# Row sums of the two longest query blocks in one accumulator each, in a two-layer transformer kernel on one Trainium2 core

## The chip, the cores and the metric

The kernel runs on one core of one Trainium2 chip. The metric is the time of one execution on the device, in microseconds (us). The kernel before was timed in three runs: 1879.6, 1879.7 and 1876.36 us, so the median is 1879.6 us. One more execution was recorded by the hardware profiler; it took 1874.3 us, and the span from its first to its last instruction is 1872.6 us.

## The reference, cut to what matters

The program computes two layers (causal attention and a mixture of experts, then a selective scan and a second mixture of experts) on 4 sequences of 1024 tokens of width 128, in float32. Only the attention of the first layer is touched. It has 16 query heads of width 64 that share 4 key and value heads (4 query heads to one key head):

```python
q = (hidden_states @ Wq).reshape(b, s, H, D).transpose(0, 2, 1, 3)     # b=4, s=1024, H=16, D=64
k = (hidden_states @ Wk).reshape(b, s, HKV, D).transpose(0, 2, 1, 3)   # HKV=4
v = (hidden_states @ Wv).reshape(b, s, HKV, D).transpose(0, 2, 1, 3)
q, k = _apply_rope(q, cos, sin), _apply_rope(k, cos, sin)
scores = jnp.einsum('bkgqd,bkpd->bkgqp', qg, k) * scale
scores = jnp.where(causal, scores, jnp.float32(-1e+30))
probs = jax.nn.softmax(scores, axis=-1)
out = jnp.einsum('bkgqp,bkpd->bkgqd', probs, v).reshape(b, H, s, D)
```

The part that the change concerns is the denominator of the softmax: for each query the sum of `exp(score - max)` over all keys up to its own.

## The kernel before, in words

**Groups.** Attention is done in 16 groups, one for each sequence and key head; a group has 4 query heads. Queries and keys are cut into 8 blocks of 128. A first pass (`s1`) makes all scores to find each row's maximum (matmuls L700 on TensorE, maximum L838 on VectorE). A second pass works on *units* `(qb, kb)`, one query block by one key block with `kb <= qb`, for the 4 heads at once, so a tile is 128 keys by 512 columns (4 heads by 128 queries). There are 36 units in a group. The second pass of group g runs beside the first pass of group g+1, and beside the rotary embedding of groups g+1 and g+2.

**One unit.** `s2`: two matmuls make the scores less the maximum (L714, L715 on TensorE, into one of 6 banks called `ring`). `exp2`: ScalarE takes the exponential into one of 9 buffers `prob` (L924); on the diagonal (`kb == qb`) GpSimd then zeroes what is above it (`affine_select`, L963). `pv`: TensorE multiplies with `v` into `ps_o` (L731).

**Row sums.** Units are gathered in *runs*. Within a run GpSimd adds the `prob` tiles: the first add makes `acc` from two tiles (L975), each later one adds a tile to `acc` (L978); there are 2 buffers `acc`. When the run is complete, TensorE multiplies `acc` with ones, once for each pair of heads (two products, L743, a step called `sum`), and adds into `ps_l`. After the last run of an odd query block ScalarE takes the logarithm and the negative exponential of `ps_l` (L928, L932, step `norm`), and VectorE multiplies `ps_o` with it (L851, step `take`). A run is a part of a *batch*: query blocks 0 and 1 form one batch, blocks 2 to 5 one each, block 6 has two batches, key blocks 0 to 3 and 4 to 6, and block 7 has two, 0 to 3 and 4 to 7. Before, a run never went beyond its batch, so query blocks 6 and 7 had two runs each. A group had 10 runs.

**Rotary embedding.** Six steps `rot` for each group (r = 0 to 5; r = 0 and 3 are keys, the others queries). TensorE projects (L682), VectorE multiplies by the cosine and swaps neighbours (L816, L817), GpSimd multiplies by the sine and adds (L945, L947). The step `split` that belongs to it makes a rounded copy on ScalarE (L903 for keys, L906 for queries) and the rest on VectorE (L827, L830). The DMAs of the queries into place follow it.

**What sets the order.** `attention_plan` gives each step a time by rule and sorts all steps by it; each engine then walks the same sorted list and issues its share in that order, without ever passing a step that waits. The second pass is spread from g+1.0 to g+1.97 in proportion to costs: 0.5 for each unit, and for the products of the batch before `0.45 * len(late) + 0.3`, where `late` holds its `pv` steps and its `sum` steps. `exp2` is placed 0.012 behind its `s2`. The steps `rot` and `split` have fixed times that don't depend on these costs. Banks of `ring` go to each step by the same times: the bank whose last holder was due earliest. Before TensorE writes to a bank it waits for the step that read that bank last. The other waits that matter: `pv` of a diagonal unit waits for the `affine_select`, and `sum` waits for the last add of its run.

Of the kernel before, what the change touches and what calls it, by code (L numbers as in the profile page):

```python
# [329 lines left out]
def load_attention(e, a, tensors, x, early, late):  # L330
# [18 lines left out]
NQB = SEQ // P  # L349
# [6 lines left out]
BATCHES = [[(0, 0), (1, 0), (1, 1)]] + [[(qb, kb) for kb in range(qb + 1)] for qb in range(2, 6)] + [  # L356
    [(qb, kb) for kb in part] for qb, parts in ((6, (range(4), range(4, 7))), (7, (range(4), range(4, 8)))) for part in parts]
# [13 lines left out]

def runs():

    out = []
    for batch in BATCHES:
        for qb in dict.fromkeys(qb for qb, _ in batch):
            out.append([unit for unit in batch if unit[0] == qb])
    return out


RUNS = runs()
RUN_OF = {unit: n for n, run in enumerate(RUNS) for unit in run}


def attention_plan():

    order = []

    def spread(steps, start, end):

        total = sum(cost for cost, *_ in steps)
        used = 0.0
        for cost, *together in steps:
            at = used + (MIDDLE * cost if len(together) > 1 else 0.0)
            order.extend((start + (end - start) * at / total, step) for step in together)
            used += cost  # L400

    for g in range(GROUPS):
        for r in range(ROTS):
            c, j = divmod(r, 1 + NPAIR)
            at = g + (ROT0, ROT1)[c] + ROT_STEP * j
            order.append((at, ("rot", g, r)))
            order.append((at + ROT_LAG, ("split", g, r)))
        order.append((g + 0.55, ("v", g)))
        for c in range(NCH):
            first = []  # L410
            for h in range(G):
                for qb in range(c * QPC, (c + 1) * QPC):
                    first.append(((qb + 1) * 0.14 + 0.3, ("s1", g, h, qb)))
            spread(first, g + (0.0, S1_HALF)[c], g + (S1_HALF, 1.0)[c])
        order.append((g + S1_HALF + 0.06, ("rows", g, 0)))
        order.append((g + 1.03, ("rows", g, 1)))
        second, late = [], []
        for j, batch in enumerate(BATCHES):
            for i, unit in enumerate(batch):
                second.append((0.5, ("s2", g) + unit))  # L420
                if late and i == min(PV_AFTER + (j == 1), len(batch) - 1):
                    second.append((0.45 * len(late) + 0.3, *late))
                    late = []
            late += [("pv", g) + unit for unit in batch] + [("sum", g, n) for n in dict.fromkeys(RUN_OF[unit] for unit in batch)]
        spread(second, g + S2_START, g + S2_END)
        order.extend((g + S2_END + LATE, step) for step in late)
        if g % HKV == 0 and g:

            for n in range(TPB // 4):
                at = g - 1.9 + 0.25 * n  # L430
                order += [(at, ("xnorm", g // HKV, n)), (at + 0.05, ("turn", g // HKV, n)), (at + 0.07, ("xout", g // HKV, n))]
        if g == GROUPS - 1:

            order.append((g + OUT, ("again", g // HKV)))
        elif g % HKV == HKV - 1:
            order.append((g + OUT - 0.001, ("again", g // HKV)))
            for n in range(TPB):
                at = g + OUT + 0.03 * n
                order.append((at, ("out", g // HKV, n)))
                order.append((at + 0.016, ("add", g // HKV, n)))  # L440
                order.append((at + 0.0199, ("stats", g // HKV, n)))
    order.append((0.5, ("gates",)))
    order += [(1.0 + 0.9 * (i - TPB) / (TILES - TPB), ("xstat", i)) for i in range(TPB, TILES)]
    order.append((1.95, ("xscale",)))

    for at, step in list(order):
        if step[0] == "s2":
            order.append((at + LAG_EXP2, ("exp2",) + step[1:]))
        elif step[0] == "sum" and RUNS[step[2]][-1][0] == RUNS[step[2]][-1][1] and RUNS[step[2]][-1][0] % 2:
            pair = RUNS[step[2]][-1][0] // 2  # L450
            order.append((at + LAG_NORM, ("norm", step[1], pair)))
            order.append((at + LAG_TAKE, ("take", step[1], pair)))
    return sorted(order, key=lambda item: item[0])


def attention(nc, sems, a, h_t, attn_t, wo, ident, eps, zeros, stats, mv, mod_t, gates, slots_in, slots_zero):
    x = h_t[:, :].rearrange("p (t n) -> p t n", n=HID)
    timed = attention_plan()
    plan = [step for _, step in timed]
    with ExitStack() as ctx:  # L460
# [2313 lines left out]
```

## Time and profile before

| | |
|---|---|
| median of three runs | 1879.6 us (1876.36 to 1879.7) |
| the profiled execution | 1874.3 us, span 1872.6 us |
| mean granted TensorE clock | 0.914 |
| attention, from the first to the last second-pass matmul | 75.6 to some 1092 us |
| busy in the span | PE 1552.5, DVE 1187.0, ACT 791.1, POOL 1264.9 us |

PE is TensorE, DVE VectorE, ACT ScalarE, POOL GpSimd. Names in a row are `out<-in`. Because matmuls are pipelined, the durations of neighbouring ones overlap; how long one really takes is read from the distance between starts. Times in rows are counted from the start of the span. A wait is named by the engine and line that released it.

### The profile page before, as it was taken

Reading aid. Unit: us, or ns where it says so; the run is one execution under the profiler, and the core shown is the slowest. Engines: PE = TensorE matmul, PEld = TensorE weight load, DVE = VectorE, ACT = ScalarE, POOL = GpSimd, SP = SyncE. Lnnn points to the kernel's source line nnn. Section 1 sums busy time; section 2 is a strip of 40 time slices with the busy share of each in tenths; the row PEclk is TensorE's granted clock in tenths of the full one; section 3 lists DMA queues with packets and bytes.
Section 4 is the critical chain, followed back from the end, with each engine's and each line's share of the span. In section 5 each row is a group of like instructions: output and inputs, shape, how many; then the busy total and the mean of one; then the engine's idle time right before and its main releaser. Section 6 shows DMA issues by size and latency. Waiting matters only on the chain. (4 is left out here: it accounts for less than half of the span.)

```text
span 1872.6 us, 26570 instructions
## 1 busy us (share of the span) xinstructions
PE 1552.5 (83%) x8882; PEld 1072.4 (57%) x8882; DVE 1187.0 (63%) x2509; ACT 791.1 (42%) x1347; POOL 1264.9 (68%) x1073
## 2 busy tenths in 40 slices
PE   5799999999999999999999989999965664356970
PEld 3455556755656765567656568888831231235970
DVE  6866676576666567666666235576659989952134
ACT  2245444344443354443444433322267855423320
POOL 5588998798888788887888753110026667658476
PEclk7799999999999999999999999999978876667995
DMA  6333322221122122122121020000036555405333
GB/s 176 70 80 79 69 56 47 46 68 35 40 63 69 29 52 68 35 52 63 35 58 45 12 67 1 1 1 1 1 101 157 143 124 139 115 26 173 98 93 85
DMA packets 93560, 125.30 MB, mean 67 GB/s; under 512 B 13664, under 2 KB 53492, under 8 KB 93424
## 3 DMA queue, kind: packets, MB, share of 16 engines
q1 hardware_dynamic: 89328, 115.58, 24.9%
q0 software_dynamic: 4096, 8.02, 1.5%
q8 instruction: 72, 1.18, 0.3%
q14 instruction: 64, 0.52, 0.1%
HBM read 56.56 MB, written 16.78 MB: 39 GB/s over the span
## 5 line engine op out<-in xcount | busy, mean ns | idle before, releaser
L838 DVE CUSTOM_DVE_ANT_0 ring<-ring,mask 128x128 f32<-128x128 f32 (+7 forms) x512 | 383.7, 769 | 186.0 <-PE ring L700 185.6
L924 ACT ACTIVATE prob<-ring 128x512 f32<-128x512 f32 x576 | 315.1, 597 | 296.6 <-PE ring L715 293.0
L978 POOL TENSOR_TENSOR acc<-acc,prob 128x512 f32<-128x512 f32 x272 | 353.3, 1299 | 72.1 <-ACT prob L924 48.3
L731 PE MATMUL ps_o<-prob,v 128*64 128x256 f32 x2304 | 282.0, 386 | 4.2 <-issue 3.8
L700 PE MATMUL ring<-k,x 128*128 128x512 f32 (+3 forms) x768 | 250.0, 405 | 36.4 <-ACT prob L924 22.1
L714 PE MATMUL ring<-x,k 128*128 128x512 f32 x576 | 258.6, 449 | 24.5 <-DVE neg_m L838 15.4
L715 PE MATMUL ring<-x,k 128*128 128x512 f32 x576 | 229.2, 398 | 0.0
L700 PEld LDWEIGHTS ring<-k,x 128*128 128x128 f32 x768 | 136.6, 197 | 143.9 <-ACT prob L924 50.5
L731 PEld LDWEIGHTS ps_o<-prob,v 128*64 128x64 f32 x2304 | 154.2, 137 | 106.3 <-issue 38.5
L975 POOL TENSOR_TENSOR acc<-prob 128x512 f32<-128x512 f32 x144 | 184.4, 1281 | 8.8 <-ACT prob L924 7.4
L945 POOL TENSOR_TENSOR other<-other,sin 128x512 f32<-128x512 f32 x96 | 136.3, 1420 | 57.1 <-DVE other L817 56.6
L714 PEld LDWEIGHTS ring<-x,k 128*128 128x128 f32 x576 | 109.3, 190 | 99.4 <-issue 44.0
L2375 POOL TENSOR_TENSOR m_hc<-m_st,m_crep 128x1024 f32<-128x1024 f32 x42 | 98.8, 2353 | 53.6 <-DVE m_st L2140 47.9
L947 POOL TENSOR_TENSOR rot<-rot,other 128x512 f32<-128x512 f32 x96 | 129.1, 1344 | 7.5
L1765 POOL TENSOR_TENSOR first_h<-first_h,e_scaled 128x512 f32<-128x512 f32 x8 | 10.3, 1285 | 174.4 <-DVE e_scaled L1647 174.4
L715 PEld LDWEIGHTS ring<-x,k 128*128 128x128 f32 x576 | 110.0, 191 | 19.9 <-issue 7.3
L830 DVE TENSOR_TENSOR rot<-rot,other 128x512 fp32r<-128x512 f32 x64 | 73.2, 1143 | 69.5 <-ACT other L906 69.5
L1633 DVE TENSOR_TENSOR e_both<-e_silu,ps_moe 128x512 f32<-128x512 f32 x88 | 60.4, 687 | 87.9 <-PE ps_moe L1477 69.4
L1717 ACT ACTIVATE e_silu<-ps_moe 128x512 f32<-128x512 f32 x88 | 52.6, 598 | 134.9 <-PE ps_moe L1477 132.2
L963 POOL TENSOR_SCALAR_AFFINE_SELECT prob<-prob 128x512 f32<-128x512 f32 x128 | 91.4, 714 | 25.8 <-ACT prob L924 24.7
L816 DVE TENSOR_TENSOR rot<-ring,cos 128x512 f32<-128x512 f32 x96 | 66.3, 690 | 58.1 <-PE ring L682 57.7
L2594 POOL DMA_INDIRECT c_got<-slots_out,f_slot x64 | 66.5, 1040 | 45.7 <-issue 39.8
(322 smaller groups left out, 3068.5 us busy)
## 6 DMA issues: line engine op xcount, KB each, us to landing
x<-other SPq DMA_DIRECT2D x256, 128.0 KB, 2.3
m_x_rep<-u_mem SPq DMA_DIRECT2D x59, 512.0 KB, 4.6
x<-rot SPq DMA_DIRECT2D x128, 128.0 KB, 2.3
slots_in<-zeros SPq DMA_DIRECT2D x2, 2048.0 KB, 8.7
slots_out<-wo SPq DMA_DIRECT2D x16, 256.0 KB, 2.5
gate<-slots_in SPq DMA_DIRECT2D x11, 256.0 KB, 3.2
m_x_rep<-u_mem SPq DMA_DIRECT2D x10, 256.0 KB, 4.2
e_w<-in_w SPq DMA_DIRECT2D x3, 704.0 KB, 6.9
```

The costliest lines, as they stand in the source:

```text
L700: mm = e.matmul(ps[:, c0:c1], x1[g % 2][:, h, qs], k1[g % 3][:, c0:c1], start=True, stop=True)
L714: e.matmul(banks(step, BANK), k1[g % 3][:, ks], x1[g % 2][:, :, qs], start=True, stop=False)
L715: e.matmul(banks(step, BANK), k2[g % 3][:, ks], x2[g % 2][:, :, qs], start=False, stop=True).then_inc(s2_pe.sem, 1)
L731: mm = e.matmul(ps_o[s * D:(s + 1) * D, qb % 2 * 2 * P:(qb % 2 + 1) * 2 * P], v[g % 2][:, kb, :], prob[i % NPROB][:, s * 2 * P:(s + 1) * 2 ...
L838: e.tensor_tensor_reduce(ps, ps, mask_1[:, SEQ - n:SEQ], 1.0, -3.0 * NEG, ALU.add, ALU.min, neg_m[g % 2][:, c, h, qb % QPC:qb % QPC + 1]). ...
L924: e.activation(prob[i % NPROB][:, :], banks(("s2",) + key, BANK), ACT.Exp, scale=-1.0).then_inc(s2_exp.sem, 1)
L945: e.tensor_tensor(other[i][:, :], other[i][:, :], sin[:, cc], ALU.mult).then_inc(rotated.sem, 1)
L947: e.tensor_tensor(rot[i][:, :], rot[i][:, :], other[i][:, :], ALU.add).then_inc(rotated.sem, 1)
L963: e.affine_select(tile[:, :], tile[:, :], [[0, G], [1, P]], ALU.is_ge, 0.0, base=0, channel_multiplier=-1).then_inc(causal.sem, 1)
L975: e.tensor_tensor(total[:, :], first[:, :], tile[:, :], ALU.add).then_inc(summed.sem, 1)
L978: e.tensor_tensor(total[:, :], total[:, :], tile[:, :], ALU.add).then_inc(summed.sem, 1)
L2375: e.tensor_tensor(hc[(b * NG + g) % NHC][:, :], st[r][:, :], crep[b % 2][:, :], ALU.mult).then_inc(hc_pool.sem, 1)
```

## The change

Runs no longer follow the batches: each query block has one run over all its key blocks. Batches stay as they are, and so do the `pv` steps. The step `sum` is placed with the batch that holds the run's last unit. A group then has 8 runs, and in query blocks 6 and 7 units (6, 4) and (7, 4), which used to open a second run, are added to the accumulator that is already there.

```diff
 def runs():
 
-    out = []
-    for batch in BATCHES:
-        for qb in dict.fromkeys(qb for qb, _ in batch):
-            out.append([unit for unit in batch if unit[0] == qb])
-    return out
+    return [[(qb, kb) for kb in range(qb + 1)] for qb in range(NQB)]
...
-            late += [("pv", g) + unit for unit in batch] + [("sum", g, n) for n in dict.fromkeys(RUN_OF[unit] for unit in batch)]
+            late += [("pv", g) + unit for unit in batch] + [("sum", g, n) for n in (RUN_OF[unit] for unit in batch if unit == RUNS[RUN_OF[unit]][-1])]
```

The program has fewer TensorE instructions and more on GpSimd, and because `len(late)` is smaller by one for two batches, all second-pass steps of a group move a little in time against the steps with fixed times. (Lines behind the first hunk have numbers smaller by 4: the first add is L971 after the change, the later ones L974, `affine_select` L959, the rotation L941 and L943, the exponential L920, `split` L902.)

GpSimd in one group, from the first add of query block 6 to its last. L945 and L947 are the rotation steps 0, 1 and 2 (by the number behind `other`); `acc0` is the sum of key blocks 0 to 3, `acc1` that of 4 to 6. Before:

```order
L975 TENSOR_TENSOR acc0<-prob3,prob4 128x512
L945 TENSOR_TENSOR other0<-other0,sin 128x512
L947 TENSOR_TENSOR rot0<-rot0,other0 128x512
L978 TENSOR_TENSOR acc0<-acc0,prob5 128x512
L945 TENSOR_TENSOR other1<-other1,sin 128x512
L947 TENSOR_TENSOR rot1<-rot1,other1 128x512
L978 TENSOR_TENSOR acc0<-acc0,prob6 128x512
L975 TENSOR_TENSOR acc1<-prob7,prob8 128x512
L963 AFFINE_SELECT prob0<-prob0 128x512
L978 TENSOR_TENSOR acc1<-acc1,prob0 128x512
L945 TENSOR_TENSOR other2<-other2,sin 128x512
L947 TENSOR_TENSOR rot2<-rot2,other2 128x512
```

The same place now:

```order
L941 TENSOR_TENSOR other0<-other0,sin 128x512
L943 TENSOR_TENSOR rot0<-rot0,other0 128x512
L971 TENSOR_TENSOR acc0<-prob3,prob4 128x512
L974 TENSOR_TENSOR acc0<-acc0,prob5 128x512
L941 TENSOR_TENSOR other1<-other1,sin 128x512
L943 TENSOR_TENSOR rot1<-rot1,other1 128x512
L974 TENSOR_TENSOR acc0<-acc0,prob6 128x512
L974 TENSOR_TENSOR acc0<-acc0,prob7 128x512
L941 TENSOR_TENSOR other2<-other2,sin 128x512
L943 TENSOR_TENSOR rot2<-rot2,other2 128x512
L974 TENSOR_TENSOR acc0<-acc0,prob8 128x512
L959 AFFINE_SELECT prob0<-prob0 128x512
```

Rotation 0 now stands ahead of the first add, there is one more add (`prob7`), and rotation 2 stands ahead of the last two adds of the block (the second of them follows the row shown last).

ScalarE in the same group, around the split of rotation 2 (`other2<-rot2`). `prob1`, `prob2` and `prob3` are the exponentials of units (7, 0), (7, 1) and (7, 2). Before:

```order
L906 ACTIVATE other1<-rot1 128x512
L924 ACTIVATE prob1<-ring 128x512
L924 ACTIVATE prob2<-ring 128x512
L906 ACTIVATE other2<-rot2 128x512
L924 ACTIVATE prob3<-ring 128x512
```

The same place now:

```order
L902 ACTIVATE other1<-rot1 128x512
L920 ACTIVATE prob1<-ring 128x512
L902 ACTIVATE other2<-rot2 128x512
L920 ACTIVATE prob2<-ring 128x512
L920 ACTIVATE prob3<-ring 128x512
```

The split of rotation 2 has moved ahead of the exponential of (7, 1).

## Rows read from the trace of the kernel before

**Rows 1.** The page: busy tenths in 40 slices of the span.

```profile
PE   5799999999999999999999989999965664356970
POOL 5588998798888788887888753110026667658476
```

**Rows 2.** Busy time by stretch: stretch, length, engines (us, instructions), clock, DMA share, GB/s.

```profile
528.70:590.40 61.70, 57.77 (x336) 37.03 (x335) 41.48 (x93) 28.09 (x54) 55.36 (x47) 1.00 0.23 52
```

**Rows 3.** Waits of TensorE in the attention, 75 to 1095 us: total, times, longest.

```profile
PE ring L700 <- ACT prob L924: 22.1, 33, 2.1
PE ring L714 <- DVE neg_m L838: 15.4, 14, 1.1
PE ring L714 <- ACT prob L924: 9.0, 13, 0.9
```

**Rows 4.** Timeline of TensorE, the second pass of group 7: start, duration, engine, instruction.

```profile
531.53 0.60 PE L743 MATMUL ps_l<-acc,v_one 128*64 128x256 f32 x4
...
542.12 0.44 PE L700 MATMUL ring<-k,x 128*128 128x384 f32 x1 [1.11 <-ACT prob L924]
...
560.18 0.40 PE L714 MATMUL ring<-x,k 128*128 128x512 f32 x1
560.42 0.39 PE L715 MATMUL ring<-x,k 128*128 128x512 f32 x1
...
581.67 0.50 PE L714 MATMUL ring<-x,k 128*128 128x512 f32 x1 [0.85 <-ACT prob L924]
...
583.50 0.50 PE L714 MATMUL ring<-x,k 128*128 128x512 f32 x1 [1.10 <-DVE neg_m L838]
...
593.21 0.60 PE L743 MATMUL ps_l<-acc,v_one 128*64 128x256 f32 x4
...
605.54 0.60 PE L743 MATMUL ps_l<-prob,v_one 128*64 128x256 f32 x4
605.97 0.60 PE L743 MATMUL ps_l<-acc,v_one 128*64 128x256 f32 x4
```

**Rows 5.** Timeline of GpSimd, the same group, query blocks 6 and 7.

```profile
566.06 1.28 POOL L945 TENSOR_TENSOR other<-other,sin 128x512 f32<-128x512 f32 x1 [0.82 <-DVE other L817]
...
568.65 1.27 POOL L978 TENSOR_TENSOR acc<-acc,prob 128x512 f32<-128x512 f32 x1
569.88 1.75 POOL L945 TENSOR_TENSOR other<-other,sin 128x512 f32<-128x512 f32 x1
...
585.00 1.27 POOL L975 TENSOR_TENSOR acc<-prob 128x512 f32<-128x512 f32 x1 [0.21 <-ACT prob L924]
...
590.83 0.64 POOL L963 TENSOR_SCALAR_AFFINE_SELECT prob<-prob 128x512 f32<-128x512 f32 x1 [0.44 <-ACT prob L924]
591.55 1.28 POOL L978 TENSOR_TENSOR acc<-acc,prob 128x512 f32<-128x512 f32 x1
592.79 1.73 POOL L945 TENSOR_TENSOR other<-other,sin 128x512 f32<-128x512 f32 x1
```

**Rows 6.** Timeline of ScalarE: the two splits that it waits for.

```profile
539.83 0.63 ACT L906 ACTIVATE other<-rot 128x512 fp32r<-128x512 f32 x1 [2.98 <-POOL rot L947]
...
580.50 0.63 ACT L906 ACTIVATE other<-rot 128x512 fp32r<-128x512 f32 x1 [2.89 <-POOL rot L947]
```

**Rows 7.** Timeline of VectorE: two of its splits.

```profile
569.39 1.08 DVE L827 SCALAR_TENSOR_TENSOR k<-rot,k 64x512 fp32r<-64x512 f32 x1
...
592.27 1.10 DVE L827 SCALAR_TENSOR_TENSOR k<-rot,k 64x512 fp32r<-64x512 f32 x1
```

**Rows 8.** Timeline of GpSimd at the end of group 14's and in group 15's second pass.

```profile
1046.50 0.63 POOL L963 TENSOR_SCALAR_AFFINE_SELECT prob<-prob 128x512 f32<-128x512 f32 x1 [1.73 <-ACT prob L924]
...
1083.93 2.70 POOL L978 TENSOR_TENSOR acc<-acc,prob 128x512 f32<-128x512 f32 x2
...
1089.66 0.63 POOL L963 TENSOR_SCALAR_AFFINE_SELECT prob<-prob 128x512 f32<-128x512 f32 x1 [0.37 <-ACT prob L924]
```

**Rows 9.** Timeline of TensorE: the last `sum` of the attention.

```profile
1091.69 0.65 PE L743 MATMUL ps_l<-acc,v_one 128*64 128x256 f32 x4 [0.69 <-POOL acc L978]
```

## The prediction

> **What bounds the kernel now.** I read the page first. In the slices of the attention (the 2nd to the 24th, some 75 to 1092 us) TensorE shows 9 tenths nearly everywhere and GpSimd 7 to 9 [rows 1]: the busiest engine is TensorE, but GpSimd is close behind it. Next comes one group by itself. The second passes of groups 1 to 13 are alike in order and nearly alike in time, so I take group 7: between its neighbours' last sums lie 593.21 - 531.53 = 61.68 us [rows 4]. In about that stretch TensorE is busy 57.77 us, GpSimd 55.36 us, and the clock is full (1.00) [rows 2]. GpSimd has 6.3 us that are not busy, and part of that is no slack: two adds that follow each other in one accumulator are a chain, and two of them take 2.70 us [rows 8], so the second starts 2.70 - 1.28 = 1.42 us behind the first, where an add that need not wait for the one before is followed after 569.88 - 568.65 = 1.23 us [rows 5].
>
> Then the waits of TensorE. In the whole attention they are small, and the largest are of one make: for ScalarE's exponential and for VectorE's maximum, 22.1, 15.4 and 9.0 us, the last two 14 and 13 times, once a group [rows 3]. In group 7 they stand at 542.12, 581.67 and 583.50 [rows 4]. What is behind them is seen on ScalarE: before both places it stood still for 2.98 and 2.89 us at a `split`, for GpSimd's rotation (L947) [rows 6], and the exponential that TensorE wanted was queued behind that split. So TensorE's pauses are GpSimd's backlog. One more number matters most. The last add of query block 7 ends at 591.55 + 1.28 = 592.83, and TensorE takes up that `sum` at 593.21 [rows 4, 5]. That is 0.38 us of slack on TensorE's own in-order queue. From rotation 0, which GpSimd begins at 566.06 after a wait for VectorE, to that add, GpSimd works through 26.77 us with hardly a pause [rows 5]. The group is a loop of two stretches: GpSimd from rotation 0 to the last add, then TensorE from the last `sum` to the next rotation 0 (61.68 - 26.77 - 0.38 = 34.53 us).
>
> **What is removed.** Two `sum` steps a group, 32 in all. One takes 605.97 - 605.54 = 0.43 us of TensorE [rows 4], so 32 x 0.43 = 13.8 us. Both lie in the batches of query blocks 6 and 7, that is inside GpSimd's stretch, where TensorE has to wait for the last add anyway. Their worth there is nothing as long as GpSimd is the later one; if it is not, it is 13.8 us.
>
> **What is added and moved, per group.** All of this is in GpSimd's stretch:
> - Two adds, for units (6, 4) and (7, 4), both in the middle of a chain: 2 x 1.42 = 2.84 us.
> - Rotation 0 now stands ahead of the first add of block 6. Before, that add filled the time in which GpSimd waited for VectorE; now it stands behind: +1.24 us. The bounds are 0 (if rotation 0 comes so early that nothing idles) and 1.42.
> - Pauses that are filled: 0.21 us before the add at 585.00, of which 0.07 is more than a chain's step, and 0.44 + 0.04 before the mask at 590.83 [rows 5]: -0.55 us.
> - The split of rotation 3 is on VectorE at 592.27 for 1.10 us, and GpSimd's instruction beside it takes 1.73 us in place of 1.28 [rows 5, 7]. With GpSimd late, that 0.45 us falls on an add before the last `sum`: +0.45 us.
>
> Sum of the stretch: 2.84 + 1.24 - 0.55 + 0.45 = 3.98 us, so 30.75 us in place of 26.77.
>
> What the loop gives back: rotation 0 is projected one unit earlier on TensorE (one `s2` less ahead of it, two matmuls at 560.42 - 560.18 = 0.24 us [rows 4]), 0.47 us. The slack of 0.38 shrinks to the least handover that `sum` steps show, some 0.05: 0.33 us. And the early wait at 542.12 hangs on rotation 5, which comes 0.33 us later against the last `sum` and 0.45 us earlier by the port that it no longer shares there: -0.12 us. The loop grows by 3.98 - 0.47 - 0.33 - 0.12 = 3.06 us.
>
> Two waits also change, inside the stretch. ScalarE's split of rotation 2 now stands ahead of the exponential of (7, 1), and by the rule for the banks TensorE's `s1` of head 3, block 4 now needs that bank; TensorE will stand there for 2 to 3 us. On the other side rotation 2 stands ahead of the last two adds of block 6, its split comes sooner, and the two waits at 581.67 and 583.50 should go. I cost both at nothing: GpSimd's backlog covers them, since it has five adds of block 7 in hand. Without that cover they are worth up to +1 us, or -1.95 us (0.85 + 1.10). The diagonal `pv` and the `sum` of block 6 will wait for the later adds; covered in the same way.
>
> The other places: 14 second passes (groups 0 to 13) have rotations in them, so 14 x 3.06 = 42.8 us. Group 14 has none, and GpSimd waited 1.73 us for its last exponential [rows 8], so there the adds are hidden and 0.86 us of products is saved. In group 15 GpSimd goes from add to add, and the last `sum` waits 0.69 us for it [rows 9]: two adds and two more chain steps, less a pause of 0.37 + 0.04 [rows 8], 2.84 + 0.38 - 0.41 = 2.8 us. Sum: 42.8 - 0.9 + 2.8 = 44.7 us. From the profiled execution's 1874.3 us this gives 1919.0 us. The median of the runs shown is 5.3 us above that execution, which would give 1924.3. I take 1922 us.
>
> The rotation's port in more detail. A split of 569.39 to 570.47 overlaps the add of 568.65 to 569.92, and the rotation behind that add, begun at 569.88, takes 1.75 us where it takes 1.28 alone [rows 5, 7]. In the Trainium skill, "SBUF — State Buffer", section "SBUF: two separate sides", the pair of ports that VectorE and GpSimd share is a lock: who starts first holds it for a whole instruction, and a VectorE instruction with two inputs in SBUF takes part. By that rule, the trace agrees: the split waits for the add and the rotation for the split. It makes each split beside a busy GpSimd cost about the same wherever it falls; if the price were instead spread over what runs beside it, the loop would grow by some 2.6 us, not 3.1.
>
> **The rivals.**
> *TensorE stays the bound.* It is busy 57.77 of 61.70 us against 55.36 [rows 2]. If GpSimd's 2.6 us more fit in its 6.3 us not busy, 13.8 us are saved, and with rotation 2 moved ahead the two late waits may go too (15.4 + 9.0 us [rows 3]): 1866 down to 1841 us. Against it: the slack of 0.38 us at the last `sum`, and that most of GpSimd's 6.3 us lie in front of rotation 0 or in handovers. The Trainium skill, "Perfetto Trace Analysis", section "Identifying the Most-Contended Engine", has the engine with the highest occupancy as the one to relieve, though it warns that TensorE's busy share misleads; taken simply, it would side with this rival.
> *Only the added work counts.* The moved rotation costs nothing, because the order before and after lets VectorE's part come early enough. Then the loop grows by 2.84 - 0.55 - 0.33 = 1.96 us, with group 15: 14 x 1.96 + 2 = some 29 us, 1903 to 1909 us.
> *GpSimd also starves.* The long stop of TensorE behind the split of rotation 2 makes the exponentials of block 7 late, so that GpSimd's backlog is used up and the filled pauses of 0.55 us come back with 0.5 to 1 us more. The loop grows by 4.1 to 4.6 us: 1935 to 1945 us. It decides once `s2` of (7, 3) comes later than GpSimd's add of (7, 2) ends.
> *Nothing to be seen.* Slack lost and products saved cancel.
> That the change doesn't do what it says is out: the order shows the adds and the moves in every group.
>
> **Chances.** My forecast 0.56, only the added work 0.20, starving 0.10, TensorE the bound 0.10, nothing 0.04. About 0.2% (3.8 us) is what a measurement can tell from no change. Faster 0.10, same 0.04, slower 0.86. The forecast's own range is 1911 to 1933; with the second case and a part of the third it is 1893 to 1938.
>
> **What would show it.** In the profile after: GpSimd with 448 adds in place of 416 and hardly a pause from rotation 0 to the last add, some 30.7 us; the last `sum` of each group waiting for GpSimd (L974), which happens in few groups before; the distance between last sums near 64.7 us; TensorE's share lower in all slices of the attention and nothing changed behind 1140 us but a shift. A wait of TensorE's first-pass matmul (L696) for an exponential near the end of block 6, and none at the later `s2`. I am wrong if the last `sum` still finds its accumulator ready, or if the distance is below 61.7 us.

## The result, and the profile after

The changed kernel takes 1914.91 us (median of four runs, 1914.21 to 1915.85) against 1879.18 us of before in the same comparison: a ratio of 1.0194, with a 95% interval of 1.0181 to 1.0207. It is slower by some 36 us; 1922 us had been predicted, in a range of 1911 to 1933. Its profiled execution has a span of 1913.2 us, 40.6 us more than that of before, where the working had come to 44.7 us. (The profiled execution of before lay 5 us below its median; that of after did not, hence 36 in the medians and 41 between the profiles.)

The same two lines of the page as in [rows 1], now after the change:

```profile
PE   5899889989988989998998989999976655455970
POOL 5588998798889688888788773201016666657476
```

TensorE now dips to 8 tenths again and again; GpSimd is as full as it was. The timeline of TensorE in group 7 (start, duration, engine, instruction), to lay beside [rows 4]:

```profile
548.48 0.65 PE L739 MATMUL ps_l<-acc,v_one 128*64 128x256 f32 x4 [0.97 <-POOL acc L974]
...
596.89 0.56 PE L696 MATMUL ring<-k,x 128*128 128x512 f32 x2 [3.01 <-ACT prob L920]
597.38 2.28 PE L727 MATMUL ps_o<-prob,v 128*64 128x256 f32 x12
599.45 1.12 PE L739 MATMUL ps_l<-acc,v_one 128*64 128x256 f32 x4
600.50 0.80 PE L710 MATMUL ring<-x,k 128*128 128x512 f32 x1
...
611.41 0.65 PE L727 MATMUL ps_o<-prob,v 128*64 128x256 f32 x4 [0.93 <-POOL prob L959]
612.76 0.65 PE L739 MATMUL ps_l<-acc,v_one 128*64 128x256 f32 x4 [0.69 <-POOL acc L974]
```

The last sums are 612.76 - 548.48 = 64.28 us apart (61.68 before), and both wait for GpSimd's last add; before, TensorE came 0.38 us after it. The pauses of 0.85 and 1.10 us are gone, and a pause of 3.01 us stands in front of the first-pass matmul of head 3, block 4. (It stands there in groups 1, 3, 7 and 11. In the other nine of groups 1 to 13 it comes a little later, 2.8 to 2.9 us for the mask of block 6, which is the first line of the waits below.) GpSimd in the same group, beside [rows 5]:

```profile
582.01 1.28 POOL L941 TENSOR_TENSOR other<-other,sin 128x512 f32<-128x512 f32 x1 [1.35 <-DVE other L813]
583.37 1.28 POOL L943 TENSOR_TENSOR rot<-rot,other 128x512 f32<-128x512 f32 x1
584.60 1.28 POOL L971 TENSOR_TENSOR acc<-prob 128x512 f32<-128x512 f32 x1
586.02 1.56 POOL L974 TENSOR_TENSOR acc<-acc,prob 128x512 f32<-128x512 f32 x1
...
590.14 2.98 POOL L974 TENSOR_TENSOR acc<-acc,prob 128x512 f32<-128x512 f32 x2
...
602.35 4.12 POOL L974 TENSOR_TENSOR acc<-acc,prob 128x512 f32<-128x512 f32 x3 [0.40 <-ACT prob L920]
...
610.27 1.09 POOL L959 TENSOR_SCALAR_AFFINE_SELECT prob<-prob 128x512 f32<-128x512 f32 x1
611.44 1.26 POOL L974 TENSOR_TENSOR acc<-acc,prob 128x512 f32<-128x512 f32 x1
```

From rotation 0 at 582.01 to the end of the last add at 612.70 are 30.69 us, where there were 26.77. The rest of the loop, from the last sum to rotation 0, is 582.01 - 548.48 = 33.53 us (34.53 before). The groups of L974 and L971 in this stretch of the profile, with 21 and 7 adds, against 17 and 9 before in a group:

```profile
L974 POOL TENSOR_TENSOR acc<-acc,prob 128x512 f32<-128x512 f32 x21 | 27.4, 1303 | 4.4 <-ACT prob L920 2.6
L971 POOL TENSOR_TENSOR acc<-prob 128x512 f32<-128x512 f32 x7 | 8.9, 1275 | 0.1
```

The waits of TensorE in the attention (total, times, longest), beside [rows 3]:

```profile
PE ps_o L727 <- POOL prob L959: 35.3, 17, 2.9
PE ring L696 <- ACT prob L920: 30.6, 31, 3.2
PE ps_l L739 <- POOL acc L974: 20.4, 28, 1.0
```

Two of the three now name GpSimd directly. One thing the prediction had not foreseen. The columns of a stretch are its length, the busy times, and then TensorE's clock; here are a piece of group 7 and one of group 8, each behind its long pause:

```profile
598.00:601.50 3.50, 3.50 (x17) 1.68 (x13) 1.45 (x4) 0.00 (x0) 3.32 (x3) 0.51 0.87 197
676.00:683.50 7.50, 6.74 (x19) 4.21 (x20) 2.65 (x6) 2.16 (x4) 6.49 (x7) 0.54 0.43 98
```

The clock is about half in both (1.2 GHz). So it is in each of groups 1 to 13, for 3.4 us in five of them and for 6.8 us in eight. It was not always full before the change either: in groups 4, 5, 8, 9 and 12 it is half for 3.4 us behind the late pauses, here in group 4:

```profile
394.30:397.70 3.40, 3.40 (x9) 2.20 (x9) 1.70 (x4) 1.19 (x2) 2.54 (x3) 0.51 0.68 156
```

In the change the `sum` at 599.45 lasts 1.12 us, and 0.60 at full clock [rows 4].

### The profile page after: what moved, and what is told of

The parts are those of the page before. It is cut to its first block and busy times, and to the rows that moved or that the text cites. A ratio compares the mean times of both kernels' runs of the same rounds, so it can differ in the third digit from the quotient of the medians.

```text
span 1913.2 us, 26364 instructions
## 1 busy us (share of the span) xinstructions
PE 1559.2 (82%) x8754; PEld 1077.8 (56%) x8754; DVE 1185.6 (62%) x2509; ACT 794.4 (42%) x1347; POOL 1301.4 (68%) x1105
## 5 line engine op out<-in xcount | busy, mean ns | idle before, releaser
L974 POOL TENSOR_TENSOR acc<-acc,prob 128x512 f32<-128x512 f32 x336 | 439.6, 1308 | 76.2 <-ACT prob L920 46.8
L920 ACT ACTIVATE prob<-ring 128x512 f32<-128x512 f32 x576 | 318.6, 596 | 310.5 <-PE ring L711 307.8
L727 PE MATMUL ps_o<-prob,v 128*64 128x256 f32 x2304 | 291.9, 393 | 39.8 <-POOL prob L959 35.3
L710 PE MATMUL ring<-x,k 128*128 128x512 f32 x576 | 276.0, 479 | 0.1
L696 PE MATMUL ring<-k,x 128*128 128x512 f32 (+3 forms) x768 | 235.2, 386 | 41.3 <-ACT prob L920 30.6
L711 PE MATMUL ring<-x,k 128*128 128x512 f32 x576 | 235.8, 409 | 0.0
L696 PEld LDWEIGHTS ring<-k,x 128*128 128x128 f32 x768 | 142.4, 199 | 124.2 <-ACT prob L920 43.7
L941 POOL TENSOR_TENSOR other<-other,sin 128x512 f32<-128x512 f32 x96 | 123.8, 1289 | 68.7 <-DVE other L813 68.6
L710 PEld LDWEIGHTS ring<-x,k 128*128 128x128 f32 x576 | 114.0, 198 | 80.4 <-issue 59.5
L971 POOL TENSOR_TENSOR acc<-prob 128x512 f32<-128x512 f32 x112 | 144.4, 1289 | 1.5
L943 POOL TENSOR_TENSOR rot<-rot,other 128x512 f32<-128x512 f32 x96 | 128.0, 1334 | 7.5
L711 PEld LDWEIGHTS ring<-x,k 128*128 128x128 f32 x576 | 114.6, 199 | 25.4 <-issue 13.3
L959 POOL TENSOR_SCALAR_AFFINE_SELECT prob<-prob 128x512 f32<-128x512 f32 x128 | 94.8, 741 | 22.6 <-ACT prob L920 21.5
L847 DVE TENSOR_TENSOR attn_t<-ps_o,inv_l 128x512 f32<-128x512 f32 x64 | 44.1, 689 | 93.0 <-ACT inv_l L928 93.0
```

The source lines that it names most:

```text
L696: mm = e.matmul(ps[:, c0:c1], x1[g % 2][:, h, qs], k1[g % 3][:, c0:c1], start=True, stop=True)
L710: e.matmul(banks(step, BANK), k1[g % 3][:, ks], x1[g % 2][:, :, qs], start=True, stop=False)
L711: e.matmul(banks(step, BANK), k2[g % 3][:, ks], x2[g % 2][:, :, qs], start=False, stop=True).then_inc(s2_pe.sem, 1)
L727: mm = e.matmul(ps_o[s * D:(s + 1) * D, qb % 2 * 2 * P:(qb % 2 + 1) * 2 * P], v[g % 2][:, kb, :], prob[i % NPROB][:, s * 2 * P:(s + 1) * 2 ...
L920: e.activation(prob[i % NPROB][:, :], banks(("s2",) + key, BANK), ACT.Exp, scale=-1.0).then_inc(s2_exp.sem, 1)
L941: e.tensor_tensor(other[i][:, :], other[i][:, :], sin[:, cc], ALU.mult).then_inc(rotated.sem, 1)
```

## The experiments

For each run the two parts of the loop in group 7 are read as above: GpSimd's stretch, the slack at the last sum, TensorE's stretch, and their sum. The kernel before has 26.77 + 0.38 + 34.53 = 61.68, the change 30.69 + 0.05 + 33.53 = 64.28 (rounded; the slack of 0.05 us is 612.76 less the end of the last add). Where a text below speaks of a mean, it is that of groups 1 to 13 of the profiled execution, read in the same way.

**The order alone** (e1_order_only). On the kernel before:

```diff
-                    second.append((0.45 * len(late) + 0.3, *late))
+                    n_late = len([s for s in late if s[0] == "pv" or RUNS[s[2]][-1][0] == RUNS[s[2]][-1][1]])
+                    second.append((0.45 * n_late + 0.3, *late))
```

> The kernel before with the order of the change and nothing else: the runs stay ten to a group (no add more on GpSimd, the products stay), but the cost of the late steps is counted as in the change, so all steps and banks stand where the change puts them. Theory (a loop of GpSimd's stretch from rotation 0 to the last add, and TensorE's from there to the next rotation 0): after the change these were 30.69 and 33.53 us; without two chained adds (2 x 1.42) the loop is some 61.4 to 61.8 us as before (61.7), so 1875 to 1885 us. Rival 'the moves are what costs' (rotations ahead of adds, the split ahead of the exponential of (7, 1)): most of the 36 us stays, 1900 to 1915 us.

Measured: 1870.74 us against 1877.31, ratio 0.9967 (0.9954 to 0.9979), 6.6 us faster than before, and outside both ranges. Timelines of TensorE and GpSimd:

```profile
529.22 0.44 PE L744 MATMUL ps_l<-acc,v_one 128*64 128x256 f32 x2 [0.73 <-POOL acc L979]
...
562.80 1.27 POOL L946 TENSOR_TENSOR other<-other,sin 128x512 f32<-128x512 f32 x1 [1.36 <-DVE other L818]
...
588.84 1.76 POOL L979 TENSOR_TENSOR acc<-acc,prob 128x512 f32<-128x512 f32 x1
590.66 0.65 PE L744 MATMUL ps_l<-acc,v_one 128*64 128x256 f32 x4 [0.73 <-POOL acc L979]
```

27.80 + 0.06 + 33.58 = 61.44 us. The moves cost GpSimd's stretch 1.0 us and give back 0.95 us of TensorE's and 0.3 us of slack: they are a small gain, not the loss. A part of the 6.6 us is the clock, which is half in one of groups 1 to 13 here, and in five before.

**The adds alone** (e2_adds_only). On the change:

```diff
-                    second.append((0.45 * len(late) + 0.3, *late))
+                    n_late = len(late) + (late[0][2] >= 6 and late[0][3] == 0)
+                    second.append((0.45 * n_late + 0.3, *late))
```

> The change with the order of before: eight runs to a group (two adds more on GpSimd, two pairs of products less), but the cost of the late steps counted as before, so nothing moves. Theory: GpSimd's stretch is 26.77 + 2.84 + up to 0.5 for chain steps and ports - 0.5 for a filled pause = some 29.4 us, TensorE's stays 34.5, the loop is 63.9 us, in all 1906 to 1915 us. Rival 'the moves are what costs': 1870 to 1885 us, since 13.8 us of products are gone and GpSimd has 6 us not busy in a group.

Measured: 1911.16 us, ratio 1.0177 (1.0161 to 1.0193): inside the theory's range, 34 us slower than before. Timelines:

```profile
547.01 0.60 PE L740 MATMUL ps_l<-acc,v_one 128*64 128x256 f32 x4
...
581.56 1.28 POOL L942 TENSOR_TENSOR other<-other,sin 128x512 f32<-128x512 f32 x1 [0.84 <-DVE other L814]
...
609.63 1.29 POOL L975 TENSOR_TENSOR acc<-acc,prob 128x512 f32<-128x512 f32 x1
```

The next last sum starts at 611.30. So 29.36 + 0.38 + 34.55 = 64.29 us: with nothing moved, nearly the whole loss is there.

**The products back** (e3_products_back). On the change, ahead of the `pv` of (6, 3) and (7, 3):

```diff
+                    if (qb, kb) in ((6, 3), (7, 3)):
+                        if qb == 6 and o_order[g, 3]:
+                            e.wait_ge(inv_act.sem, o_order[g, 3])
+                        for s in range(2):
+                            e.matmul(ps_l[s * D:(s + 1) * D, qb % 2 * 2 * P:(qb % 2 + 1) * 2 * P], v_one[:, :],
+                                     prob[i % NPROB][:, s * 2 * P:(s + 1) * 2 * P], start=True, stop=True)
```

> The change with the two pairs of products with ones issued again in their old places (their result is overwritten by the real ones), 32 pairs of 0.43 us. Theory: they lie in GpSimd's stretch, so only group 14 and nothing else grows: 1914 to 1918 us. Rival 'TensorE's work sets the pace': 1915 + 13.8 = 1929 us.

Measured: 1917.93 us, ratio 1.0218 (1.0202 to 1.0234), 3 us above the change, not 14. (The change was timed in another comparison; by the two ratios, 1.0218 and 1.0194, it is 4.5 us.) In the profiled executions the last sum of the attention comes 1132.06 - 1130.83 = 1.2 us later, 0.9 of them in group 14; the other 2 us lie behind the attention, where nothing was edited. In group 7 the distance is 64.33 us with the products and 64.28 without. So the 13.8 us of products that the change removes were worth some 1 to 5 us.

**The adds left out** (e4_adds_out). On the change: `NO_ADD = ((6, 4), (7, 4))`, and GpSimd passes over these units.

```diff
-                    if unit == run[0]:
+                    if unit == run[0] or unit in NO_ADD:
                         continue
```

> The change without the two added adds: the tiles of units (6, 4) and (7, 4) are left out of the row sums; the order and the removed products stay as in the change. Theory: GpSimd's stretch 30.69 - 2.84 = 27.9 us, loop 61.4 us, and the removed products give something only in groups 14 and 15: 1872 to 1880 us. Rival 'TensorE's work sets the pace': 13.8 us less than the run with the order alone.

Measured: 1879.22 us, ratio 1.0003 (0.9991 to 1.0016). The two adds a group are worth 36 us by this (44 us against the run with the order alone, and 34 us in the order of before). The rival, 13.8 us below the run with the order alone, is out: it is 8 us above. In group 7 the loop is 28.57 + 0.06 + 33.56 = 62.19 us, 0.75 us more than with the order alone. There the exponential of (7, 3) came 0.9 us later, in a stretch in which TensorE's clock was half, behind a pause of 1.80 us; with the order alone that pause was 1.42 us and the clock stayed up.

This run has a comparison within itself. Groups 7 and 11 have the same steps in the same order, and all but the same pause at the same place (1.80 and 1.78 us). Behind it the clock fell in one and not in the other:

```profile
577.83 0.56 PE L699 MATMUL ring<-k,x 128*128 128x512 f32 x2 [1.80 <-ACT prob L923]
842.37 0.56 PE L699 MATMUL ring<-k,x 128*128 128x512 f32 x2 [1.78 <-ACT prob L923]
```
```profile
578.80:582.20 3.40, 3.40 (x16) 1.70 (x13) 1.59 (x4) 0.00 (x0) 3.17 (x4) 0.50 0.85 192
843.30:846.70 3.40, 2.84 (x19) 1.66 (x16) 1.63 (x4) 0.41 (x1) 3.17 (x4) 1.00 0.90 205
```

GpSimd's stretch is 28.57 us in group 7 and 27.74 in group 11: these 3.4 us at half the clock go with 0.83 us more. Over groups 1 to 13 the stretch is 27.73 to 27.75 us in the five groups whose clock stayed up and 28.56 to 30.66 in the eight others; in the mean it is 0.68 us longer than with the order alone, and TensorE's stretch is the same. Over 13 groups that is 8.9 us, about the 8 us by which this kernel is slower than the order alone, though it has less to do.

**The split put back** (e5_split_later). On the change:

```diff
-            order.append((at + ROT_LAG, ("split", g, r)))
+            order.append((at + ROT_LAG + (0.006 if r == 2 else 0.0), ("split", g, r)))
```

> The change, with the split of rotation 2 put back behind the exponential of (7, 1) on ScalarE (and nothing else moved on TensorE, VectorE or GpSimd). In the change TensorE pauses 3.0 us at the first-pass matmul of head 3, block 4, for that exponential. Theory (GpSimd's stretch is what counts): the pause only moves to the mask or the last add of block 6, some 2 to 3 us later in the same stretch; 1908 to 1917 us. Rival 'GpSimd starves behind that split': the stretch gives back 1 us or more a group, 1895 to 1900 us.

Measured: 1919.36 us, ratio 1.0233 (1.0218 to 1.0248): no gain at all, and a little above the theory's range. TensorE's timeline in group 7, and the clock of the stretch behind:

```profile
599.74 1.12 PE L727 MATMUL ps_o<-prob,v 128*64 128x256 f32 x4 [2.83 <-POOL prob L959]
```
```profile
599.00:606.00 7.00, 5.94 (x17) 3.67 (x18) 3.19 (x7) 1.35 (x3) 6.14 (x6) 0.54 0.49 113
```

The pause has moved on to the mask of block 6 and is nearly as long. In nine of the groups 1 to 13 it was there in the change already, so the run tests the split in the other four. Of the 4 us more than in the change, a part lies behind the attention, where nothing was edited, and a part goes with the clock, which is now half for 6.8 us in twelve of the groups (in eight before the edit). Among groups with 6.8 us of it GpSimd's stretch is alike, 31.00 to 31.66 us here and 31.06 to 31.71 in the change. So the place of the split costs nothing that these runs show; GpSimd is late in any case.

**The pause filled** (e8_pause_filled, then e9_pause_filled_12). On the change, in TensorE's stream ahead of the matmul that pauses; `range(12)` first, then `range(6)`:

```diff
+                if kind == "s1" and key[0] and key[1:] == (G - 1, QPC):
+                    e.wait_ge(inv_act.sem, o_order[key[0] - 1, 3])
+                    for _ in range(12):
+                        for s in range(2):
+                            e.matmul(ps_l[s * D:(s + 1) * D, 0:2 * P], v_one[:, :], cos[:, 0:2 * P], start=True, stop=True)
```

> The change, with 24 products whose result is overwritten issued on TensorE ahead of its 3.0 us pause near the end of block 6 (2.6 us of work in each group that has one). In the profile after the change TensorE's granted clock goes to 1.2 GHz for some us behind that pause, and in the groups where it stays there longest GpSimd's stretch is 31.5 us in place of 30.7. Theory 'the lower clock is a part of the price': the clock stays up there, the stretch is 30.2 to 30.7 in all groups, 1902 to 1911 us. Theory 'the clock plays no part': 1915 us or more.

Measured: 1926.27 us, ratio 1.0265 (1.0251 to 1.0278). The products were sized at half of what they take: 5.4 us, longer than the pause. So as a test of the time this run says nothing.

> As the kernel with the filled pause, but 12 products, not 24: the 24 took 5.4 us and not 2.6, longer than the pause of 3.0 us, so that run added TensorE work to the stretch. 12 take 2.7 us and fit. Theory 'the lower clock is a part of the price of the change': the clock stays at 2.4 GHz in nearly all groups, GpSimd's stretch is 30.2 to 30.7 us in every group, 1903 to 1912 us. Theory 'the clock plays no part': 1915 us or more, stretches of 30.6 to 31.7 as they were.

Measured: 1921.45 us, ratio 1.0238 (1.0214 to 1.0263). The fill, the pause that is left, and the clock of two stretches:

```profile
595.83 2.81 PE L671 MATMUL ps_l<-cos,v_one 128*64 128x256 f32 x24
598.93 0.56 PE L701 MATMUL ring<-k,x 128*128 128x512 f32 x2 [0.29 <-ACT prob L925]
```
```profile
596.00:601.00 5.00, 4.64 (x38) 2.52 (x36) 2.58 (x4) 1.60 (x3) 4.84 (x5) 1.00 0.60 139
613.00:618.00 5.00, 4.14 (x16) 2.40 (x17) 0.97 (x3) 1.80 (x4) 4.46 (x5) 0.66 0.00 2
```

One half of the expectation held: the clock is full behind the fill, and GpSimd's stretch is 30.43 to 30.50 us in each of groups 1 to 13, against 30.55 to 31.71 and a mean of 31.14 in the change. The other half fell: the time did not drop. The clock now went down at other places, in group 7 around its last sums (the records show half of it from 549.3 and from 614.1 us on), and TensorE's stretch was longer there (34.90 us, not 33.53; 37.62 and 36.76 in the mean). Ahead of that place TensorE now pauses longer, 1.51 us in place of 0.93:

```profile
613.16 0.65 PE L732 MATMUL ps_o<-prob,v 128*64 128x256 f32 x4 [1.51 <-POOL prob L964]
```

And group 14, which has no pause to fill, took 59.65 us, not 55.38; that alone is 4.3 of the 6.5 us by which this kernel is slower than the change.

**Shorter runs.** If GpSimd is the late one, the change in the other direction should gain. Three kernels cut the second batches of blocks 6 and 7 once more, so that GpSimd has fewer adds and TensorE more products: both in the order of the change (e6_short_runs), both in the order of before (e7_short_runs_old_order), and in that order one at a time.

```diff
-            out.append([unit for unit in batch if unit[0] == qb])
+            run = [unit for unit in batch if unit[0] == qb]
+            out += [run[:2], run[2:]] if run[0][1] == 4 else [run]
...
-                    second.append((0.45 * len(late) + 0.3, *late))
+                    n_late = len([s for s in late if s[0] == "pv"]) + len(dict.fromkeys(s[2] for s in late if s[0] == "pv"))
+                    second.append((0.45 * n_late + 0.3, *late))
```

> The order of the change (which alone took 1870.7 us, against 1877.3 of before), and shorter runs in place of longer ones: the second batches of query blocks 6 and 7 are two runs each (4 and 5 | 6; 4 and 5 | 6 and 7), so GpSimd has two adds less and TensorE two pairs of products more than before (0.43 us each). Theory: GpSimd's stretch falls by up to 2.8 us from 27.8; TensorE's three pauses in it (1.4 + 0.5 + 0.7 us) shrink to what 0.9 us more products leave, so 0.8 to 1.8 us a group are gained: 1842 to 1862 us. Rival 'TensorE's work sets the pace': 32 x 0.43 = 13.8 us slower than the order alone, 1884 us.

Measured: 1855.52 us against 1875.37, ratio 0.9889 (0.9874 to 0.9903): inside the theory's range, and 15 us below the order alone.

> The same shorter runs in the order of before. Theory: TensorE's two pauses there (0.85 + 1.10 us) shrink, 0 to 1.1 us a group gained: 1860 to 1877 us. Rival 'TensorE's work sets the pace': 1877 + 13.8 = 1891 us.

Measured: 1851.20 us, ratio 0.9871 (0.9857 to 0.9885), 24 us faster than before and better than forecast. The loop is 25.15 + 0.81 + 34.35 = 60.31 us. (Its last two sums stand in one row; the last begins 0.43 us behind the start of the row.) TensorE's two pauses are gone from its list of waits:

```profile
519.22 1.03 PE L745 MATMUL ps_l<-acc,v_one 128*64 128x256 f32 x8
...
553.99 1.27 POOL L947 TENSOR_TENSOR other<-other,sin 128x512 f32<-128x512 f32 x1 [0.84 <-DVE other L819]
...
577.86 1.28 POOL L977 TENSOR_TENSOR acc<-prob 128x512 f32<-128x512 f32 x1
...
579.53 0.82 PE L745 MATMUL ps_l<-acc,v_one 128*64 128x256 f32 x6
```
```profile
PE ring L702 <- ACT prob L926: 19.9, 33, 2.0
PE ps_o L733 <- issue: 3.8, 10, 0.5
```

I had forecast up to 1.1 us a group; it gained 1.37 in group 7. TensorE does 0.86 us more products and pauses 1.95 us less, which is 1.1, and the rest is not traced. In the mean of groups 1 to 13 the gain is 1.81 us: with the pauses gone the clock stays up in all of them, and GpSimd's stretch is 25.02 to 25.18 us everywhere, where before it was 26.68 to 26.81 in eight groups and 27.77 to 28.13 in the five with the lower clock.

Then the cut in block 7 alone (`run[0] == (7, 4)` in the condition) and in block 6 alone (`run[0] == (6, 4)`):

> The order of before, shorter runs in query block 7 alone (4 and 5 | 6 and 7): one add less, one pair of products more. Theory: TensorE's pauses of 0.85 and 1.10 us hang on rotation 2, which stands ahead of block 7's adds, so they stay; the last sum waited for nothing before. The loop grows by 0.43 us less what the slack leaves: 1875 to 1884 us, no gain. Rival 'each add less on GpSimd is worth the same': half of the 24 us of the run with both, 1863 us.

Measured: 1880.20 us against 1878.39, ratio 1.0016 (1.0003 to 1.0028). Its waits keep both pauses, in full:

```profile
PE ring L716 <- DVE neg_m L840: 15.4, 14, 1.1
PE ring L716 <- ACT prob L926: 9.0, 13, 0.8
```

> The same in query block 6 alone (4 and 5 | 6). Theory: the add that goes stood ahead of rotation 2, so both pauses go (1.95 us a group) for 0.43 us of products, until the last sum waits for GpSimd again: 1850 to 1858 us, nearly all of the gain of both. Rival 'each add less is worth the same': 1863 us.

Measured: 1865.35 us, ratio 0.9937 (0.9920 to 0.9954). That is above both times that were forecast. Counted from this comparison's kernel before it is a gain of 13 us, which is what the rival gave (12) and not the theory's 17 to 25; but the rival gave 12 us to block 7 as well, and that gained nothing. Both pauses are gone, and the last sum now waits for GpSimd (slack 0.05 us), so a part of the gain is capped: 25.76 + 0.05 + 35.00 = 60.81 us. So where an add stands decides: none of it gained in block 7 alone, half in block 6 alone, and all only with both. The expectation named that limit and put it too far off.

## Why the prediction was right, and where its terms were off

**The removed products.** Predicted worth nothing inside GpSimd's stretch, 0.86 us in group 14. Right in the main: issuing them again cost 1 to 5 us of 13.8, and group 14 went from 55.99 to 55.38 us.

**The two adds.** Predicted +2.84 us a group. In group 7 the kernels with and without them in the order of the change differ by 30.69 - 27.80 = 2.89 us in GpSimd's stretch, in the order of before by 29.36 - 26.77 = 2.59 us. Shown from both sides. In both pairs a part of it is the clock: it is half for some us in each group that has the adds.

**The moved rotation.** Here sizes were off. I had +1.24 us in GpSimd's stretch and -0.47 us for a rotation that is projected one unit earlier. The order by itself added 1.03 us to the stretch, with port and pauses in it, and TensorE's stretch fell by 0.95 to 1.00 us, about twice my figure: in the timelines of both kernels the projection comes 1.06 us earlier after the last sum (31.99 and 30.93 us). Some 0.3 us of that were gained up to the `sum` of block 4 (25.83 and 25.56 us after the last sum), where I had seen no difference, and the rest behind it. So by my two terms the order was a loss of 1.24 - 0.47 = 0.77 us a group (0.44 with the slack that it uses up), and measured alone it is a gain of 0.24 us in group 7, of 0.48 in the mean, and of 6.6 us in all. In groups 4, 8 and 12 TensorE's stretch grew by 0.5 to 1.2 us, in 5 and 9 it fell by 2.0.

**Filled pauses and the port.** Predicted -0.55 and +0.45 us. The mask of (7, 7) takes 1.09 us in place of 0.64, as forecast for the instruction there; two adds of block 6 take 0.28 us longer each, and rotation 1 (0.47 us before) and an add of block 7 (0.25 us) are no longer lengthened. In sum the stretch bears 1.46 us of such excess in place of 1.17: +0.29 us. The pauses were filled but one of 0.40 us appeared at 602.35, for the exponential of (7, 3): the rival "GpSimd also starves" in small.

**The loop.** Predicted 64.7 us between last sums; 64.28 in group 7, and +2.66 us in the mean of groups 1 to 13 against a forecast of 3.06. GpSimd's stretch was forecast as 30.75 us and is 30.69. Groups 0 to 13 together grew by 1029.54 - 992.54 = 37.0 us (the times of their last sum), and 42.8 had been forecast. Luck has a part in this. I took group 7 for all of groups 0 to 13 and called them nearly alike in time. Before, the last sums of groups 4, 8 and 12 lie 74.6 to 75.0 us behind those of the group ahead, those of 5 and 9 64.5 to 64.6. The loop grew by 3.9 to 4.4 us in the first three and by 0.1 and 0.8 in the other two; only the mean is near the forecast. Also the terms that were wrong offset each other: the order gave where I had it take, and the clock took.

**The covered waits.** The pause of 2 to 3 us behind the split of rotation 2 was 3.01 us, and the two late pauses went, as said. Putting the split back gained nothing, so what waits behind the pause is covered in fact. But the pause was not free, as I had it: the clock falls behind it, and that price stands in no term of mine.

**Groups 14 and 15.** Predicted -0.9 and +2.8 us, measured -0.6 and +2.75 (43.16 to 45.91 us).

**The rivals.** TensorE as the bound is out by three experiments (products back, adds out, shorter runs). "Only the added work counts" (1903 to 1909 us) was nearer for the wrong reason: the order was not free, it gained. What hid that gain in the changed kernel is in part the clock. Behind the long pause TensorE's clock is half in every group from 1 to 13, and then GpSimd waits for exponentials: the stretch is 30.55 to 30.69 us in the five groups with 3.4 us at half clock and 31.06 to 31.71 in the eight with 6.8. Filling the pause brought all to 30.46, 0.69 us a group in the mean, or some 9 us. The kernel before pays this price too. With shorter runs in block 7 alone (e10_short_7_only) the clock stays up in groups 4, 5, 8, 9 and 12, and GpSimd's stretch is 26.66 to 26.81 us there, 1.0 to 1.5 us less than before, 6.3 us in sum. So my estimate is that of the 36 us some 9 - 6 = 3 are the clock, and the rest is the added work less what the order gives back. It is no more than an estimate, since the clock also acts on TensorE's own stretch, as the kernel with the filled pause shows.

**The ports.** Four instructions of GpSimd last longer than alone beside a split of VectorE: by 0.28 us (1.56 for 1.28, the add at 586.02), by 0.28 us again (in the pair at 590.14, 2.98 us for two adds 1.42 us apart, which alone would take 2.70), and twice by 0.45 us (1.09 for 0.64, the masks of block 6 and of block 7 at 610.27). Each of them begins while the split is still running. The Trainium skill, "SBUF — State Buffer", section "SBUF: two separate sides", has the pair of ports that VectorE and GpSimd share as a lock held for a whole instruction. That GpSimd's next instruction is held up each time agrees with it; no run here takes the lock apart from the rest.

## What to carry to other kernels

Where two engines hand work to each other in a loop, find the point at which one waits for the other and measure the slack there; work taken from the engine that waits was worth little here (1 to 5 us of 13.8), and work put on the other was paid nearly in full. A chained add costs its whole step (1.42 us), and what it costs the kernel depends on what is queued behind it: taking one add away gained nothing in one block and 13 us in another. And read more than one round of the loop: group 7 was near the mean growth, and five others were not. The busier engine (94% against 90% here) was not the one to relieve: fewer adds on GpSimd for more products on TensorE is the version that beats both kernels, 1851 us.

## What the runs showed of the hardware

TensorE's granted clock went from 2.4 to 1.2 GHz in the middle of an attention in which it is over 90% busy, in the groups looked at in or right behind a pause in which it waited for another engine: in group 7 of the change one of 3.01 us, before the change in five groups one of 1.1 us (in three of them with one of 0.8 us ahead of it). Then the next matmuls took about double (a `sum` of 1.12 us in place of 0.60). The same pause does not always do it: with the adds left out the clock fell behind 1.80 us in group 7 and not behind 1.78 us in group 11, and before the change it stayed up in group 7 behind 0.85 and 1.10 us. The 3.4 us at half clock in group 7 went with a GpSimd stretch that was 0.83 us longer. The mean clock of the whole execution was 0.914 before and 0.898 after the change; with shorter runs, where the two late pauses are gone, it was 0.919. So a pause that is covered as a wait can still lengthen the path of an engine that waits for TensorE later.
